# A causal attention takes its output projection, the second normalisation and the gate logits into its own loop, and the linear output is written anew

## The reference

```python
# linear attention, 16 heads of 16; its result joins later
q_feat, k_feat = elu(q * SCALE) + 1, elu(k) + 1
kv = einsum('bhtd,bhtv->bhdv', k_feat, v);  k_sum = k_feat.sum(axis=2)
denom = maximum(einsum('bhtd,bhd->bht', q_feat, k_sum), 1e-6)
out = einsum('bhtd,bhdv->bhtv', q_feat, kv) / denom[..., None]
out = out @ W_out
# causal softmax attention, 16 heads of 16, then a mixture of experts
attn = einsum('bhqk,bkhd->bqhd', probs, v).reshape(Bb, Tt, d) @ Wproj
x = x + attn
h2 = layernorm(x, ln2_g, ln2_b)
gates = softmax(h2.reshape(-1, d) @ Wgate)
# top 2 of 8 experts by gates, capacity by position, rows scattered to their expert
```

## Time and profile before

| what | us |
|---|---|
| median of three runs | 3463.48 |
| the profiled execution | 3469.7 |
| its span, first to last instruction | 3468.1 |
| TensorE busy | 2942.6 (85%) |
| VectorE busy | 2099.1 (61%) |
| ScalarE busy | 1588.5 (46%) |
| GpSimd busy | 1048.7 (30%) |
| mean granted clock of TensorE | 0.917 |

### The profile page before, as it was taken

One profiled execution on the slowest core, in us unless ns is written; L12 is line 12 of the kernel. 1 busy time (PEld: TensorE's weight loads), 2 busy tenths in 40 slices (PEclk: granted clock), 3 DMA queues, 4 the chain that ended last, 5 costly groups with the idle time before them and its releaser, 6 DMA issues. The chain is left out here.

```text
span 3468.1 us, 50053 instructions
## 1 busy us (share of the span) xinstructions
PE 2942.6 (85%) x17923; PEld 1370.3 (40%) x17923; DVE 2099.1 (61%) x4629; ACT 1588.5 (46%) x2665; POOL 1048.7 (30%) x498
## 2 busy tenths in 40 slices
PE   4777599999999956279999958959999999999967
PEld 2444333333333335156666634423333333333315
DVE  4778598998999724120000046528878778778615
ACT  1443246777677722032222224414565665665650
POOL 1233100000000010600000022105677777777764
PEclk8898689999999975699999979968999999999988
DMA  7111402110121070221212045460202202202028
GB/s 239 49 48 57 101 7 41 41 39 21 39 41 44 11 115 24 104 73 55 91 54 91 18 135 160 142 171 7 50 17 59 56 11 59 56 17 53 8 51 217
DMA packets 178246, 231.85 MB, mean 67 GB/s; under 512 B 29146, under 2 KB 135581, under 8 KB 175360
## 3 DMA queue, kind: packets, MB, share of 16 engines
q1 hardware_dynamic: 161040, 197.46, 21.3%
q0 software_dynamic: 8704, 22.27, 1.9%
q10 hardware_dynamic: 8304, 9.51, 1.4%
HBM read 138.51 MB, written 93.06 MB: 67 GB/s over the span
## 5 line engine op out<-in xcount | busy, mean ns | idle before, releaser
L832 POOL TENSOR_TENSOR at_probs<-at_probs 128x2048 f32<-128x2048 f32 (+3 forms) x208 | 734.2, 3531 | 332.3 <-ACT at_probs L870 224.0
L870 ACT ACTIVATE at_probs<-at_st 128x512 f32<-128x512 f32 (+3 forms) x1280 | 591.8, 541 | 446.3 <-PE at_st L938 252.1
L371 DVE TENSOR_REDUCE at_part<-at_s 128x1 f32<-128x512 f32 (+3 forms) x1280 | 689.4, 602 | 82.5 <-PE at_s L409 43.6
L353 ACT ACTIVATE at_probs<-at_st 128x1024 f32<-128x1024 f32 (+3 forms) x640 | 541.6, 895 | 289.4 <-PE at_st L436 147.2
L894 DVE TENSOR_REDUCE at_part<-at_s 128x1 f32<-128x512 f32 x768 | 498.9, 685 | 132.9 <-PE at_s L930 129.2
L930 PE MATMUL at_s<-at_kT,at_qT 96*128 96x512 f16 (+3 forms) x1280 | 387.9, 360 | 29.4 <-DMA at_kT<-klo 18.8
L938 PE MATMUL at_st<-at_qT,at_kT 98*128 98x512 f16 (+3 forms) x1280 | 373.6, 354 | 31.8 <-DMA at_qT<-at_strip 21.6
L409 PE MATMUL at_s<-at_kT,at_qT 48*128 48x512 f16 (+3 forms) x1280 | 359.9, 367 | 31.0 <-DMA at_qT<-qhi 13.0
L489 PE MATMUL at_acc<-at_probs,at_v 128*32 128x512 f32 (+3 forms) x2560 | 305.2, 550 | 8.9 <-ACT at_otile L340 8.8
L888 DVE CUSTOM_DVE_ANT_0 at_s<-at_s,at_later 128x384 f32<-128x384 f32 (+3 forms) x512 | 247.8, 499 | 95.8 <-PE at_s L930 95.0
L993 PE MATMUL at_acc<-at_probs,at_v 128*32 128x512 f32 (+3 forms) x2560 | 288.6, 538 | 9.7 <-ACT at_otile L846 9.5
(11 more groups left out here) (289 smaller groups left out, 3657.0 us busy)
## 6 DMA issues: line engine op xcount, KB each, us to landing
at_v<-v SPq DMA_DIRECT2D x16, 1024.0 KB, 15.9
att<-at_otile SPq DMA_DIRECT2D x64, 256.0 KB, 2.4
lin_w<-in_W SPq DMA_DIRECT2D x16, 1024.0 KB
exp_in<-all_zeros SPq DMA_DIRECT2D x1, 8192.0 KB, 29.0
v<-pr_vt SPq DMA_DIRECT2D x32, 256.0 KB, 3.1
ex_xin<-exp_in SPq DMA_DIRECT2D x8, 1024.0 KB, 6.3
exp_out<-ex_ot POOLq DMA_DIRECT2D x32, 256.0 KB, 2.5
v<-p_vt SPq DMA_DIRECT2D x32, 256.0 KB, 4.7
```

What stands on the lines that cost most here:

```text
L353: act.activation(probs[:, quad % RING, heads_down * p:heads_down * (p + 1), off:QB], st_ps[n % st_slots][:, :, off:QB], ACT.Exp, scale=EXP ...
L371: dve.tensor_reduce(part[:, w % 2, qt * HG + h, j:j + 1], s_ps[n % S_SLOTS][:, 0:width], AX.X, ALU.max).then_inc(item_free, 1)
L832: pool.tensor_tensor(total, total, probs[:, slots.slot[quad], :, off:QB], ALU.add).then_inc(add_done, 1)
L870: act.activation(probs[:, slots.slot[quad], h, off:QB], st_ps[n % ST_SLOTS][:, off:QB], ACT.Exp, scale=EXP_SCALE).then_inc(exp_done, 1)
```

## The change

Inside the first attention there are new events. The planner puts **NV** 6 us behind the eviction of a unit of an odd group: SP has moved the two groups' output tiles, by eight DMAs each of 16 rows, into `heads_out` (results) and `heads_sum` (sums) in SBUF; ScalarE makes the inverse as exp(-ln), GpSimd refines and multiplies. For each block of a batch, once its four groups are done, **A0** and **A1** project two token tiles each into a score slot and VectorE adds them to x and takes bn_stats; **LN** makes the statistics on GpSimd (root by exp(-0.5 ln) on ScalarE) and normalises four tiles there; **TZ** transposes them into an ST slot, **LG** multiplies with the gate weights. The normalised rows are stored to `z_rows` in DRAM and loaded again by `route`. `after_attention`, `row_statistics` and `gate_logits` are gone. In both attentions the first part of the shift is made by a scalar_tensor_tensor with a tensor of zeros in place of a tensor_scalar. `linear_out` is unrolled, by pairs of tiles, with constant waits, reads the features in place, takes the maximum with a tensor of 1e-6, and has four numerator slots, two for transposes and two for the projection. The scatters also wait for `z_all`.

```diff
+                then.append((act + 6000, "NV", (g, u)))
+                then.sort()
...
+        if kind == "NV":
+            act = max(act, ready) + 1200
+            if g % HG == HG - 1:
+                then.append((act + 9000, "A0", (g, u)))
+        elif kind in ("A0", "A1"):
+            start = max(pe, ready, slot_free[n_item % s_slots] + 60) + (SWITCH if mode == 16 else 0)
+            pe = issue = start + 1710
+            dve = max(dve, pe + 220) + 650 + 900
+            slot_free[n_item % s_slots] = dve - 900
+            n_item += 1
+            mode = 32
+            then.append((ready, "A1", (g, u)) if kind == "A0" else (dve + 7000, "LN", (g, u)))
+        elif kind == "LN":
+            act = max(act, ready) + 600
+            then.append((act + 7000, "TZ", (g, u)))
...
+                if g >= 2:
+                    before = [x for x in joined if x[1] == u and x[0] < g - g % 2][-1]
+                    sp.wait_ge(divided, joined.index(before) + 1)
+                if g >= HG:
+                    sp.wait_ge(stat_done, 4 * rounds.index((HG - 1, u)) + 4)
+                for part in (1, 0):
+                    for h in range(HG):
+                        src = otile[32 * h + hd * part:32 * h + hd * (part + 1), n % 2, :]
+                        row = 64 * (g % 2) + hd * h
+                        dst = (heads_sum[row:row + hd, u, :] if part else
+                               heads_out[row:row + hd, g % HG // 2, cols])
+                        sp.dma_start(dst, src).then_inc(moved[n % 2], 16)
...
+                if ev[0] == "LG":
+                    t, m = first_tile(ev[1]), rounds.index(ev[1])
+                    while ended:
+                        move(ended.pop(0)[0])
+                        moved_units += 1
+                    sp.wait_ge(z_ready, 4 * m + 4)
+                    sp.dma_start(z_rows[t:t + 4, :, :].rearrange("t p d -> p t d"), z[:, m % 2, :, :]
+                                 ).then_inc(z_stored[m % 2], 16)
...
+                if ev[0] == "NV":
+                    g, u = ev[1]
+                    held = heads_out[:, g % HG // 2, u * QB:(u + 1) * QB]
+                    m = joined.index(ev[1])
+                    pool.wait_ge(inverted, m + 1)
+                    if m:
+                        pool.wait_ge(divided, m)
+                    step(tt(rest[:, :], heads_sum[:, u, :], inverse[:, :], ALU.mult))
+                    step(ts(rest[:, :], rest[:, :], -1.0, 2.0, ALU.mult, ALU.add))
+                    step(tt(rest[:, :], rest[:, :], inverse[:, :], ALU.mult))
+                    tt(held, held, rest[:, :], ALU.mult).then_inc(divided, 1)
...
+                while ended and ev[0] in ("NV", "LN", "TZ", "LG"):
+                    evict(ended.pop(0))
+                    evicted += 1
+                if ev[0] == "NV":
+                    g, u = ev[1]
+                    m = joined.index(ev[1])
+                    for unit in ((g - 1, u), (g, u)):
+                        t = place_of[unit]
+                        act.wait_ge(moved[t % 2], MOVES * (t // 2 + 1))
+                    if m:
+                        act.wait_ge(divided, m)
+                    act.activation(inverse[:, :], heads_sum[:, u, :], ACT.Ln).then_inc(log_done, 1)
+                    act.wait_ge(log_done, m + 1)
+                    act.activation(inverse[:, :], inverse[:, :], ACT.Exp, scale=-1.0).then_inc(inverted, 1)
...
-                    dve.tensor_scalar(shift[:, b, :, 0], rowmax[:, b, :], -1.0 / MSHIFT, None,
-                                      ALU.mult).then_inc(hi_done, 1)
+                    dve.scalar_tensor_tensor(out=shift[:, b, :, 0], in0=rowmax[:, b, :],
+                                             scalar=-1.0 / MSHIFT, in1=nothing[:, :],
+                                             op0=ALU.mult, op1=ALU.add).then_inc(hi_done, 1)
...
+                elif ev[0] in ("A0", "A1"):
+                    y = 2 * (ev[0] == "A1")
+                    t, m = first_tile(ev[1]) + y, rounds.index(ev[1])
+                    dve.wait_ge(item_ready, n + 1)
+                    dve.tensor_tensor(x_all[:, t:t + 2, :], x_all[:, t:t + 2, :],
+                                      s_ps[n % S_SLOTS][:, :].rearrange("p (t d) -> p t d", t=2),
+                                      ALU.add).then_inc(item_free, 1)
+                    n += 1
+                    dve.wait_ge(item_free, n)
+                    if m:
+                        dve.wait_ge(var_ready, m)
+                    for k in range(2):
+                        dve.bn_stats(stats[:, y + k, :], x_all[:, t + k, :]).then_inc(stat_done, 1)
...
+                elif ev[0] in ("A0", "A1"):
+                    unit, y = ev[1], 2 * (ev[0] == "A1")
+                    pe.wait_ge(after_ld, 64)
+                    pe.wait_ge(divided, joined.index(unit) + 1)
+                    pe.wait_ge(item_free, n - S_SLOTS + 1)
+                    for k in range(2):
+                        at = unit[1] * QB + (y + k) * P
+                        for f in range(NF):
+                            mm = pe.matmul(s_ps[n % S_SLOTS][:, k * D:(k + 1) * D],
+                                           heads_out[:, f, at:at + P], w_proj[:, f, :],
+                                           start=f == 0, stop=f == NF - 1)
+                    mm.then_inc(item_ready, 1)
+                    n += 1
...
+            dve.memset(least[:, :], 1e-6).then_inc(least_ready, 1)
+            dve.wait_ge(heads_ld, 16)
             for n in range(B * NF):
                 dve.tensor_tensor(kvd[:, n, :], kv_sum[:, n, :], heads[:, :], ALU.mult).then_inc(kv_ready, 1)
...
+            for t in range(NT):
+                dve.wait_ge(num_ready, t + 1)
+                s = num_ps[t % 4][:, 0:NF * WID].rearrange("p (c n) -> p c n", c=NF)
+                d = den[:, t % 2, :].rearrange("p (c h) -> p c h", c=NF)
+                dve.tensor_tensor(d, s[:, :, P:WID], least[:, :].rearrange("p (c h) -> p c h", c=NF),
+                                  ALU.max).then_inc(raised, 1)
+                dve.wait_ge(raised, t + 1)
+                dve.reciprocal(d, d).then_inc(inverted, 1)
+                if t >= 8:
+                    dve.wait_ge(tr_ready, (t - 8) // 2 + 1)
+                dve.wait_ge(inverted, t + 1)
+                dve.tensor_tensor(nrm[:, t % 8, :].rearrange("p (c h d) -> p c h d", c=NF, h=8),
+                                  s[:, :, 0:P].rearrange("p c (h d) -> p c h d", h=8),
+                                  d.unsqueeze(3).to_broadcast([P, NF, 8, 16]), ALU.mult).then_inc(nrm_ready, 1)
...
+            for t in range(4):
+                numerator(t)
+            for m in range(PAIRS):
+                turn(m)
+                for t in (2 * m + 4, 2 * m + 5):
+                    if t < NT:
+                        numerator(t)
+                if m:
+                    output(m - 1)
+            output(PAIRS - 1)
...
+            sp.dma_start(z_all[:, :, :], z_rows.rearrange("t p d -> p t d")).then_inc(z_ld, 16)
...
-            narrow_attention(nc, "at0", C, *qk[0][0], *qk[0][1], groups(v[0]), att[0])
-            after_attention(nc, W, att[0], all_sums[0], inverse[0], x_all, stats)
-            row_statistics(nc, "rs1", stats, mean, rstd)
+            logits = lin.sb("logits", [P, NT, E], F32)
+            narrow_attention(nc, "at0", C, W, *qk[0][0], *qk[0][1], groups(v[0]), x_all, z_rows, logits)
             z_all = lin.sb("z_all", [P, NT, D], F32)
-            logits = lin.sb("logits", [P, NT, E], F32)
+            z_ld = lin.sem("z_ld")
             scatter_at = lin.sb("scatter_at", [P, 2, NT], U32)
             sent = lin.sem("sent")
-            gate_logits(nc, C, W, x_all, mean, rstd, z_all, logits)
-            route(nc, C, W, logits, scatter_at, gather_at, gate)
+            route(nc, C, W, logits, scatter_at, gather_at, gate, z_rows, z_all, z_ld)
             X, load_weights = expert_operands(lin, W)
 
             linear_out(nc, C, W, qf_all, kv_sum, s_out,
```

More of the change, by code:

```diff
@@ L113, in lead @@
         return place[first] + of_unit / count[first] - place[unit] - kc / (4 * unit[1] + 4)
-    while at < len(ahead) or n_pair < len(pairs) or n_quad < len(steps):
+    while at < len(ahead) or n_pair < len(pairs) or n_quad < len(steps) or evictions or then:
+        if n_quad == len(steps):
+            evict(1e18)
+        if then and (then[0][0] <= pe or n_quad == len(steps)):
+            later()
+            continue
         choice = []
@@ L2124, in route @@
-def route(nc, C, W, logits, scatter_at, gather_at, gate):
+def route(nc, C, W, logits, scatter_at, gather_at, gate, z_rows, z_all, z_ld):
     with Ctx(nc, "rt") as c:
```

494 lines of the change are left out of this document (231 added, 263 removed).

## The result

The kernel after takes 3494.3 us (median of six, 3486.6 to 3499.2) against 3468.4 us for before beside it: a ratio of 1.0072, 95% interval 1.0051 to 1.0093. On another chip the pair stood at 1.0050 (1.0033 to 1.0067). It is slower, by 0.7% on the one chip and 0.5% on the other, where 29.8 us less had been forecast, and it lies outside the range.

What follows compares the result with a forecast made beforehand. TensorE and VectorE were taken as full in the first attention, with half-idle chains behind it. 118.3 - 32.5 - 23 - 38 - 3 + 8 = 29.8 us less, and 6.2 from profiled to timed, gave 3433.7 us; range 3376 to 3468.

Steps and rivals of the forecast that it cites:

- Removed stages: Between first attention and routing: the two stages from 1240.9 to 1359.2 us go, all on the path, minus 118.3 us.
- Rounds: First attention: projection, statistics and gate logits in eight rounds, five counting at 6.5 us each, plus 32.5 us (17 to 42).
- Joinings: First attention: sixteen joinings of two head groups fit into idle ScalarE and GpSimd, costing nothing as long as nobody waits.
- Holds: First attention: ScalarE waits for output-tile moves before the logarithm, longest at three group ends, plus 23 us (0 to 60).
- rival 2: First attention: all sixteen joinings hold ScalarE, 6.5 us of path each, 104 us in place of 23, 3515 us; chance 0.12.
- The tail: Behind the attention's last eviction: the last block's chain of 32.2 us plus 6 for queueing, plus 38 us (30 to 55).
- Reload of the rows: Routing: normalised rows, 4 MB, come back from DRAM and the scatters wait for them, plus 3 us (0 to 13).
- Linear output: Linear output: late TensorE signals stay until scatters end, then six blocks take 6.9 us, not 8.15; minus 8 us (0 to 9).
- rival 1: Linear output: loops and register waits cause the stall, which goes; 50 us gained in place of 8, 3392 us; chance 0.27.
- The shift: Both attentions: the rewritten shift instruction on VectorE is still held by GpSimd passes, so the gain is nothing.
- Rival 3: Second attention: the rewritten shift is not held by GpSimd, 14 us come through, 3420 us; chance 0.05.
- Rival 4: Behind the first attention: rounds pile up there, taking as long as the two old stages, 3459 us; chance 0.06.

Runs made afterwards that it cites:

- later joinings: Kernel after with each joining placed 16 us behind its eviction in the written order, not 6: 3460.5 us, 0.9953 of before.
- the move to VectorE: Kernel after with joinings at 16 us and GpSimd's work behind the last score tile given to VectorE: 0.9928 of before, on another chip 0.9907.
- both: Kernel after with joinings at 16 us and all eight rounds behind the attention's last step: last eviction at 1247.7 us; no whole time given.
- rounds at the end: Kernel after with all eight rounds behind the attention's last step, joinings unmoved: 1.0363 of before, last eviction at 1301.8 us.

## Why the prediction was wrong, point by point

**Bounds.** TensorE and VectorE are as good as full in the attention, so that added work or a hold lengthens it: this held in every version.

**Removed stages, minus 118.3.** They went, whole.

**Rounds, plus 32.5 (17 to 42).** Too low, by 7 us in one comparison and 19 in the other. A round's TensorE work inside the attention is 3.7 + 1.1 + 1.95 = 6.75 us:

```profile
927.12 3.72 PE L669 MATMUL at_s<-at_w_proj,at_heads_out 128*128 128x256 f32 x16
...
931.37 1.09 PE L680 MATMUL at_st<-all_identf,at_z 128*128 128x128 f32 x8
...
935.19 1.95 PE L688 MATMUL at_st<-at_w_gate,at_hT 128*128 128x8 f32 x16
```

The logits are near their lower bound, at a high clock; five rounds did fall inside, and the projection of a sixth. But nothing of them was hidden behind VectorE: taking them out gave 39.5 us, as much as the 40.0 us that TensorE is busy with them, and 51.2 us where no wait for moves was in the way, for one round less. The reason I had for hiding a part, that only one of the two full engines counts at a time, is not borne out.

**Joinings, nothing "as long as nobody waits".** ScalarE's and GpSimd's own work for them cost 10.9 us at most, against the spread of 9.4: nearly right, and small beside the waits.

**Holds, plus 23 (0 to 60).** The step that failed. The waits themselves were foreseen where the loads stand in front: 9 us in three groups, and the trace has 7.8, 10.6 and 10.4. For the thirteen others I had 5 us on the path, and the trace has 15.9 us of waits, among them 6.5 us at 1076.5: the tile was evicted at 1061.2, but SyncE's queue stood in front of the strip copies of the next block, which it issued at 1067.45, and the moves followed at 1069.99 (eight issues at 0.62 us). I had looked only at the loads as what the moves are queued behind. The larger error is the price. I let ScalarE's slack absorb a third of each wait, 6 us on the path of 9. In fact the path pays them nearly in full or more: 25.6 us for 28.7 us less of waits where only the moves' place changed; 42.4 for 43.6 with later joinings (37.0 by the start of the routing, and 36.1 for 42.6 between the two traces of one chip); 54.1 for 42.5 with the rounds out. That is 0.85 to 1.27 us for each, where two thirds had been counted, and the term is 36 to 54 us in place of 23. A quarter of idle time on ScalarE is no cover for a single wait of 8 us: its exponentials empty two PSUM slots, and once these are full TensorE stands still (12.7 us busy of the 20 around the first long wait) and works on at a lower clock afterwards. The prediction named the two slots and priced neither the stop nor the clock.

That is also **rival 2**, in its mechanism if not in its size. It had a deciding point of 3.3 us per joining. Measured were 42.4 / 16 = 2.7 to 54.1 / 16 = 3.4 us each, not the 6.5 it assumed for every one, and only nine of the sixteen waited at all. So the holds took 42 to 54 of the 53 us that the gain would have been without them, and that the kernel is slower took the rounds and the tail too. I had put a chance of 0.12 on it, and its argument against (a store outside the loads lands after 2.5 us) was true of one store in an empty queue and said nothing of SyncE's order.

**The tail, plus 38 (30 to 55).** 47.6 us without the barrier (51.1 - 3.5), 9.6 more, inside the bounds. Three rounds hung there, as foreseen, one of them with its projection done, and GpSimd works them off in order, 13.4 us for a joining and a round (1344.26 to 1357.63) where 11.6 had been counted: the z tiles took 4.85 us alone. TensorE's fills wait for them and then run for the most part at the lower level of the clock:

```profile
1342.00:1392.00 50.00, 23.35 (x104) 20.74 (x104) 5.76 (x12) 8.46 (x19) 30.64 (x56) 0.64 0.12 38
```

GpSimd is busy for 30.6 of 50 us; the queueing that I gave 6 us is the term that was short, as the move to VectorE shows (13.4 us back).

**Reload of the rows, plus 3 (0 to 13).** Nothing, for the 4 MB landed 14.8 us after their issue, 283 GB/s, where I had taken a rate between 128 and 160: the first scatter starts 1.0 us behind the stage's first load (1412.75), and 0.9 before (1379.76).

**Linear output, minus 8 (0 to 9).** 13.8 here, 13 to 15 by itself. The mechanism was right (late counts stay, the pace behind them improves), the pace was not: I took TensorE's sum of 6.9 us for a block as its least, and the new form does it in 6.2. The Trainium skill (Runtime: NRT & Kernel Launch, Instruction fetch mechanics), which I weighed for rival 1, names a taken branch as the cause of a fetch stall. If that were the stall of this stage, the unrolled form would be free of it. The trace shows otherwise: waits named remote of up to 43.5 us stay with no loop left. **Rival 1** is out, though not every chip has the stall to begin with.

**The shift.** Held as before: the group of the second attention reads

```profile
L1132 DVE SCALAR_TENSOR_TENSOR at_shift<-at_rowmax,at_nothing 128x16 f16<-128x16 f32 x32 | 54.3, 1696 | 1.1
```

and 54.0 us at 1688 ns before. **Rival 3** is out. With the rule of the Trainium skill named for it (SBUF — State Buffer, Who interferes with whom) the trace agrees. **Rival 4** did not come: five of eight rounds lie inside.

**The sum.** Forecast 29.8 less, measured 20.8 more in the traces, 50.6 apart: holds and rounds 49.0, tail 9.6, reload -3, linear output -5.8, the rest of the kernel 1.7, which makes 51.5; the 0.9 by which this is too much is 0.3 in the routing and 0.6 at the seams (122.4 less 118.3 is 4.1, where the barrier was counted at 3.5). Taken in the order before, both, rounds at the end, after, the 49.0 are 10.9 for the joinings' own work, 31.1 for the holds (54.1 less 23) and 7.0 for the rounds (39.5 less 32.5). What I should have seen from the trace of before is that a full TensorE, fed from two slots by a queue in which a wait on a DMA is placed, pays nearly each microsecond of that wait.

## What to carry to other kernels

A wait on a transfer that is put into the queue of an engine which feeds a full one cost nearly its whole length here (0.85 to 1.27 us for each), however much idle time that engine had on average: compare the wait with the buffers between the two engines, not with the share of idle time. Before a transfer is waited for, read what stands in front of it on its issuing queue, loads and other waits alike; putting the consumer 10 us later in the written order brought back 34 to 41 us of the kernel's time, with 5 us of lengthened tail already taken off. Work that was taken into a full stage to get rid of an idle one was paid there at full price (39.5 us for 40.0 us of TensorE's time), and its last pieces, which nothing hides, gained 13.4 us by going to an idle engine that is faster at them.

## What the runs showed of the hardware

The linear output's lateness depends on the chip. The same code, with the same scatters beside it, takes 131 us on some chips, with counts of TensorE seen by VectorE and ScalarE up to 43.5 us late, and 90 us on another, with none over 2.1 us. Before takes 3468, 3477 and 3482 us where it is seen, and 3423 and 3428 us on the two chips where no trace showed it (the second only with the scatters held), a difference of 41 to 58 us, larger than the 21 that the whole change costs. How much of it is the linear output's is shown for the new form alone (131 against 90 us). On such chips I expect the new form to gain nothing, since both end inside the scatters; that is argued, not measured. What makes the counts late is open.

Around stops of TensorE of 6 to 10 us (5.8, 7.5, 10.0 and 10.1) in a stage that was at full clock there before, the granted clock was 0.69 to 0.83 over 20 us. Summed over stretches of 20 us as length times (1 - granted clock), it comes to 62 us in after, 69 with rounds at the end, 49 and 35 in the two versions without holds, and 30 in before; five traces of before's own attention gave 30 to 43. Most of before's 30 lies in its first 100 us. So the holds and the clock go together, but no run kept TensorE busy through a hold, and how much of the loss is the clock's is not shown.
